# Making three quarters of two expert stages' norms in the attention stage ahead, and ending the expert blocks without GpSimd's drain

## The reference

```
def _layernorm(x, axis=-1, eps=1e-05):
    m = jnp.mean(x, axis=axis, keepdims=True)
    v = jnp.var(x, axis=axis, keepdims=True)
    return (x - m) / jnp.sqrt(v + eps)

x = x + _L0_xattn_ref(_layernorm(x), ctx, ctx, ...)   # 16 heads of 16 over ctx
x = x + _L0_ffn_ref(_layernorm(x), ...)               # experts choose tokens
x = x + _L1_xattn_ref(_layernorm(x), ctx, ctx, ...)   # 16 heads of 64 over ctx
x = x + _L1_ffn_ref(_layernorm(x), ...)               # each token's best 2 of 8 experts
x = x + _L2_xattn_ref(_layernorm(x), ctx)
x = x + _L2_ffn_ref(_layernorm(x), ...)               # quantised weights
x = x + _L3_xattn_ref(_layernorm(x), ctx, ctx, ...)
x = x + _L3_ffn_ref(_layernorm(x), ...)               # quantised inputs and weights
```

```
# _L0_ffn_ref: 16 experts, each takes its best 64 of 512 tokens
router_logits = jax.nn.silu(hidden_states @ router_w1) @ router_w2
expert_probs = jax.nn.softmax(router_logits.transpose(0, 2, 1), axis=-1)
expert_weights, token_indices = jax.lax.top_k(expert_probs, cap)
...
# _L1_ffn_ref: 8 experts of width 256 or 512
probs = jax.nn.sigmoid(logits.astype(jnp.float32))
topw, sel = jax.lax.top_k(probs, TOP_K)
```

## Time and profile before

| | before |
|---|---|
| median of 3 runs | 1683.46 us (1682.42 to 1688.7) |
| profiled execution: its own time | 1683.53 us |
| its span | 1681.7 us |
| mean granted TensorE clock | 0.918 |
| first VectorE work of f1 | 235.80 us |
| first VectorE work of a2 | 593.28 us |
| first work of f3 | 1014.15 us |
| first fetch of a4 | 1222.64 us |

### The profile page before, as it was taken

The page is one execution under the profiler, slowest core; times in us unless marked ns, Lnnn a source line. Parts: engine busy times, 40 slices in busy tenths (PEclk is TensorE's granted clock), DMA queues, the critical chain, the costliest instruction groups (busy, mean ns, idle before and its releaser), DMA issues. The chain is left out here.

```text
span 1681.7 us, 29336 instructions
## 1 busy us (share of the span) xinstructions
PE 1415.6 (84%) x9650; PEld 1138.7 (68%) x9650; DVE 1078.5 (64%) x2487; ACT 836.1 (50%) x1944; POOL 488.6 (29%) x428
## 2 busy tenths in 40 slices
PE   5899974999999749999999995699856897888885
PEld 4666542888888647888888873599744786555553
DVE  4677643666666537777787765644366753688886
ACT  2466541544544437666677764255423543455551
POOL 2112011577777610000000004255412311134343
PEclk8899876999999979999999997699978997799997
DMA  4322124456556345544554434122173002222110
GB/s 144 122 87 84 50 101 163 113 140 163 134 136 164 60 126 141 127 115 114 133 131 104 108 120 133 34 77 77 60 227 105 1 0 62 74 78 74 60 52 26
DMA packets 140109, 168.91 MB, mean 100 GB/s; under 512 B 20136, under 2 KB 131880, under 8 KB 137448
## 3 DMA queue, kind: packets, MB, share of 16 engines
q1 hardware_dynamic: 115000, 131.42, 26.7%
q0 software_dynamic: 16032, 27.01, 7.5%
q10 hardware_dynamic: 8976, 9.17, 1.8%
HBM read 75.66 MB, written 24.12 MB: 59 GB/s over the span
## 5 line engine op out<-in xcount | busy, mean ns | idle before, releaser
L1131 ACT ACTIVATE a_probT<-a_t 128x512 f32<-128x512 f32 x256 | 151.6, 602 | 164.6 <-PE a_t L860 138.5
L941 DVE TENSOR_REDUCE a_nmax<-a_s 128x2 f32<-128x512 f32 x256 | 170.9, 685 | 92.2 <-PE a_s L856 92.0
L63 POOL TENSOR_TENSOR a_rstd<-a_veps,minus_half 128x2 f32<-128x2 f32 x32 | 23.2, 724 | 507.1 <-DVE a_veps L57 507.1
L856 PE MATMUL a_s<-a_ka,a_qa 48*128 48x256 f32 x512 | 123.2, 342 | 44.8 <-DVE a_nmax L941 21.2
L856 PEld LDWEIGHTS a_s<-a_ka,a_qa 48*128 48x128 f32 x512 | 78.6, 202 | 105.3 <-issue 61.4
L441 DVE TENSOR_REDUCE a_nmax<-a_score 128x2 f32<-128x512 f32 x128 | 88.0, 687 | 86.7 <-PE a_score L334 86.6
L536 ACT ACTIVATE a_prob<-a_score,a_nmax 128x256 f32<-128x256 f32 x256 | 120.3, 481 | 34.4 <-DVE a_nmax L441 34.3
L1665 POOL DMA_INDIRECT x_rows<-f_hn,f_scatter_row x60 | 129.9, 2164 | 16.4 <-issue 16.4
L860 PE MATMUL a_t<-a_qa,a_ka 50*128 50x256 f32 x512 | 123.2, 339 | 2.2 <-DMA a_qa<-a_m_lo 1.2
L1608 ACT ACTIVATE f_gate<-f_gate 128x512 f32<-128x512 f32 x64 | 38.3, 599 | 129.0 <-PE f_gate L1411 111.0
L1521 DVE TENSOR_TENSOR f_y<-f_gate,f_value 128x512 f32<-128x512 f32 x64 | 44.0, 688 | 80.4 <-PE f_value L1411 78.4
(11 more groups left out here) (385 smaller groups left out, 4414.3 us busy)
## 6 DMA issues: line engine op xcount, KB each, us to landing
area_odd<-in_L_experts SPq DMA_DIRECT2D x15, 1536.0 KB, 6.8
a_k_hi<-a_k_fresh_hi SPq DMA_DIRECT2D x128, 128.0 KB, 2.4
a_ctxT<-in_ctxT SPq DMA_DIRECT2D x64, 128.0 KB, 2.6
a_ka<-a_k_hi SPq DMA_DIRECT2D x128, 64.0 KB, 2.6
a_k_lo<-a_k_fresh_lo SPq DMA_DIRECT2D x64, 128.0 KB, 2.4
a_q<-a_q_fresh_hi SPq DMA_DIRECT2D x64, 128.0 KB, 2.4
a_q<-a_q_fresh_lo SPq DMA_DIRECT2D x64, 128.0 KB, 2.4
a_qa<-a_q_hi SPq DMA_DIRECT2D x120, 64.0 KB, 2.6
```

Source lines behind the costliest of these rows:

```text
L856: last_s = nc.tensor.matmul(ps_s[i][:, half, :], qa[rows, u % RING, j, half * P:(half + 1) * P], ka[rows, u % RING, j, :], start=True, sto ...
L941: nc.vector.tensor_reduce(nmax[:, u % 2, :, i * PPU + j], ps_s[i][:, :, :], AX.X, ALU.max, negate=True).then_inc(sem["nmax"], 1)
L1131: nc.scalar.activation(probT[:, t % NPT, i, :, :], ps_t[i][:, :, :], ACT.Exp).then_inc(sem["exp"], 1)
```

## The change

1. The norms of groups 0 to 2 of f1 are made in a0's last batch: stats at steps T = 56, 59, 62, apply at 57, 60, 63, each behind what VectorE does in that step; the power on GpSimd, in the step of the stats. Those of f3 are made in a2's last batch: stats at s = 8, 10, 12, apply at s = 9, 11, 13. They go into buffers (`chip.early`) that overlay a0's and a2's own norm and context buffers, which the last batch has done with; the first stats wait for that. The x that is normed is complete for those groups, since batches 0 to 5 are added by then.
2. f1 and f3 norm group 3 alone. TensorE's transposes and SP's writes of h of groups 0 to 2 wait for nothing of the norm any more.
3. f1's three early roundings on ScalarE move from in front of the copies to behind `keep_hidden(0)`, `(1)` and `(2)`.
4. f3's twelve roundings get another order and place: one per group between copy and sigmoid, the other eight after the last sigmoid. VectorE's first two subtractions stand ahead of the first scores and after the last copy of a transpose. GpSimd's memsets come ahead of its power, and its six subtractions wait for one norm, not four, and by the new order.
5. The Blocks of f1 and f3 end without GpSimd's drain. `scatter_row`, which its last scatters read, moves out of f1's own buffers.
6. In a2 the buffer `fresh` is placed ahead of `k_hi`.

```diff
+def early_stats(nc, dve, chip, sem, g):
+    norm_stats(nc, dve, chip.x, sem, chip.early, g * GT, GT, g, g * GT)
+def early_rstd(nc, pool, chip, sem, g):
+    norm_rstd(nc, pool, chip, sem, chip.early, GT, g, g * GT)
+def early_apply(nc, dve, chip, sem, g):
+    norm_apply(nc, dve, chip.x, sem, chip.early, g * GT, GT, g, chip.early.hn[:, g * GT:(g + 1) * GT, :], sem["hn"], g * GT)
...
# a2, VectorE
+            def norms_ahead(s):
+                g, odd = divmod(s - NU // 2, 2)
+                if 0 <= g < chip.early_groups:
+                    if odd:
+                        early_apply(nc, dve, chip, e_sem, g)
+                    else:
+                        if g == 0:
+                            for what in "kq":
+                                dve.wait_ge(*placed(B - 1, what, NKQ - 1))
+                            dve.wait_ge(sem["vb"], B * NV)
+                        early_stats(nc, dve, chip, e_sem, g)
...
+                    if not more:
+                        norms_ahead(s)
...
# a2, GpSimd, behind its last norm_rstd
+            for g in range(chip.early_groups):
+                early_rstd(nc, pool, chip, e_sem, g)
...
# a0
+    NORMS_AHEAD = 8 * (B - 1)
+    def norms_ahead(T, at):
+        n, off = divmod(T - NORMS_AHEAD - at, 3)
+        return n if start and off == 0 and 0 <= n < chip.early_groups else None
...
# a0, VectorE
+                if norms_ahead(T, 0) is not None:
+                    g = norms_ahead(T, 0)
+                    if g == 0:
+                        for kind in "qkv":
+                            dve.wait_ge(sem[projected[kind]], B)
+                        dve.wait_ge(sem["ctx_lo"], B)
+                    early_stats(nc, dve, chip, e_sem, g)
+                if norms_ahead(T, 1) is not None:
+                    early_apply(nc, dve, chip, e_sem, norms_ahead(T, 1))
...
# f1 and f3
-        block = ctx.enter_context(nc.Block())
+        block = ctx.enter_context(nc.Block(no_gpsimd_drain=True))
...
# f1 and f3, SP and TensorE
-                sp.wait_ge(sem["hn"], g + 1)
+                if g >= E_G:
+                    sp.wait_ge(sem["hn"], g - E_G + 1)
...
# f1, ScalarE
-            for n in range(3):
-                high_weights(0, 0, n)
             keep_hT(0)
             for g in range(1, GROUPS):
                 keep_hT(g)
                 keep_hidden(g - 1)
+                high_weights(0, 0, g - 1)
...
# f3
+    ROUNDED = [0, 6, 1, 7, 2, 8, 3, 9, 4, 5, 10, 11]
...
# f3, VectorE
+            for g in range(E_G, GROUPS):
+                norm_stats(nc, dve, chip.x, sem, nb, g * GT, GT, g - E_G, g * GT)
+                norm_apply(nc, dve, chip.x, sem, nb, g * GT, GT, g - E_G, hn[:, g * GT:(g + 1) * GT, :], sem["hn"], g * GT)
+            low_weights(POOL_PIECES)
             keep_scores(0)
             keep_scores(1).then_inc(sem["score"], 1)
             dve.wait_ge(sem["hTp"], GROUPS * KC)
             nc.vector.tensor_copy(hT[:, 1, 1, :], ps_T[1][:, :]).then_inc(sem["hT_last"], 1)
-            for n in range(POOL_PIECES, POOL_PIECES + 2):
-                low_weights(n)
+            low_weights(POOL_PIECES + 1)
...
# f3, ScalarE
-            for n in range(3):
-                high_weights(n)
             for g in range(GROUPS):
                 keep_hT(g)
-                if g + 1 < GROUPS:
-                    high_weights(3 * g + 3)
+                high_weights(ROUNDED[g])
                 keep_scoreT(g)
-                if g + 1 < GROUPS:
-                    for n in range(3 * g + 4, 3 * g + 6):
-                        high_weights(n)
+            for n in ROUNDED[GROUPS:]:
+                high_weights(n)
...
# f3, GpSimd
             def low_weights(n):
-                pool.wait_ge(sem["W_hi"], n + 1)
+                pool.wait_ge(sem["W_hi"], ROUNDED.index(n) + 1)
...
-            pool.wait_ge(sem["hn"], GROUPS)
+            pool.wait_ge(sem["hn"], GROUPS - E_G)
...
+        chip.early_groups = GROUPS - 1
```

More of the change, by code:

```diff
@@ L72, in norm_apply, with early_norms @@
     last.then_inc(sem_out, 1)
+def early_norms(nc):
+    at = -(-nc.sbuf_base // 32) * 32
+    buf, words = Bufs(), 0
+    for name, shape in (("stats", [P, TILES, 6]), ("mv", [P, TILES, 2]), ("veps", [P, TILES]), ("rstd", [P, TILES]), ("hn", [P, TILES, D])):
+        size = 1
+        for n in shape[1:]:
+            size *= n
+        alias = nc.alloc_sbuf_tensor_at(f"early_{name}", shape, F32, offset=at + 4 * words)
+        if name == "stats":
+            buf.stats = alias
+        elif name == "mv":
+            buf.mv = alias
+        elif name == "veps":
+            buf.veps = alias
+        elif name == "rstd":
+            buf.rstd = alias
+        else:
+            buf.hn = alias
+        words += size
+    buf.words = words
+    return buf
+def early_stats(nc, dve, chip, sem, g):
[4 more added lines that the diff above has]
+    norm_apply(nc, dve, chip.x, sem, chip.early, g * GT, GT, g, chip.early.hn[:, g * GT:(g + 1) * GT, :], sem["hn"], g * GT)
 def stage_semaphores(nc, chip, stage, names):
@@ L182, in head_attention @@
         ctx_hi, ctx_lo = sb("ctx_hi", [P, KC, S], F32R), sb("ctx_lo", [P, KC, S], F32R)
+        fresh = {what: [sb(f"{what}_fresh_{n}", [P, CPR, S], F32R) for n in ("hi", "lo")] for what in "kq"}
         k_hi = sb("k_hi", [P, H, S], F32R)
@@ L185, in head_attention @@
         q2 = sb("q2", [P, H, S], F32R)
-        fresh = {what: [sb(f"{what}_fresh_{n}", [P, CPR, S], F32R) for n in ("hi", "lo")] for what in "kq"}
         vb = sb("vb", [P, TB, E])
@@ L701, in narrow_head_attention @@
                                "score nmax st exp pv osb qrow0 qrow1 qrow2 qrow3 krow0 krow1 krow2 krow3 mrow0 mrow1"
+                               + (" e_stats e_aggr e_veps e_rstd e_hn" if start else "")
                                + (" l_stats l_aggr l_veps l_rstd l_hn amax qscale iscale v grid unit low big t_ up upp step rows_ "
@@ L704, in narrow_head_attention @@
         l_sem = {name: sem["l_" + name] for name in "stats aggr veps rstd hn".split()} if linear else None
+        e_sem = {name: sem["e_" + name] for name in "stats aggr veps rstd hn".split()} if start else None
         projected = {"hT": "hTp", "q": "qp", "k": "kp", "v": "vp", "mT": "mTp", "OT": "OTp", "BT": "BTp", "out": "outp", "XT": "XTp", "lin": "linp"}
@@ L1293, in pb @@
             return ctx.enter_context(nc.psum_tensor(f"{stage}_{name}", shape, F32))
-        nb = norm_buffers(nc, ctx, stage, TILES)
-        hn = sb("hn", [P, TILES, D])
+        sb("early", [P, chip.early.words])
+        nb, hn = chip.early, chip.early.hn
+        E_G = chip.early_groups
         hT = sb("hT", [P, KC, B * S])
@@ L1684, in pair_of @@
                     scatter(q, not more and q == 1)
-            for g in range(GROUPS):
-                norm_rstd(nc, pool, chip, sem, nb, GT, g, g * GT)
+            for g in range(E_G, GROUPS):
+                norm_rstd(nc, pool, chip, sem, nb, GT, g - E_G, g * GT)
             pool.wait_ge(sem["next"], 1)
@@ L2159, in pb @@
             return ctx.enter_context(nc.psum_tensor(f"{stage}_{name}", shape, F32))
-        stats = sb("stats", [P, TILES, 6])
-        mv = sb("mv", [P, TILES, 2])
-        veps = sb("veps", [P, TILES])
-        rstd = sb("rstd", [P, TILES])
-        hn = sb("hn", [P, TILES, D])
+        sb("early", [P, chip.early.words])
+        nb, hn = chip.early, chip.early.hn
+        E_G = chip.early_groups
         hT = chip.spare_words.rearrange("p (q k s) -> p q k s", q=2, k=KC)
@@ L2353, in then @@
                 dve.wait_ge(sem["top"], step[0])
-            def statistics(g):
-                tiles = range(g * GT, (g + 1) * GT)
-                for t in tiles:
-                    last = nc.vector.bn_stats(stats[:, t, :], chip.x[:, t, :])
-                last.then_inc(sem["stats"], 1)
-                nc.vector.memset(veps[:, g * GT:(g + 1) * GT], EPS)
-                dve.wait_ge(sem["stats"], g + 1)
-                for t in tiles:
-                    last = nc.vector.bn_aggr(mv[:, t, :], stats[:, t, :])
-                last.then_inc(sem["aggr"], 1)
-                dve.wait_ge(sem["aggr"], g + 1)
-                these = slice(g * GT, (g + 1) * GT)
-                nc.vector.tensor_tensor(veps[:, these], veps[:, these], mv[:, these, 1], ALU.add).then_inc(sem["veps"], 1)
-            def normalise(g):
-                dve.wait_ge(sem["rstd"], g + 1)
-                for t in range(g * GT, (g + 1) * GT):
-                    last = nc.vector.tensor_scalar(hn[:, t, :], chip.x[:, t, :], mv[:, t, 0:1], rstd[:, t:t + 1], ALU.subtract, ALU.mult)
-                last.then_inc(sem["hn"], 1)
             def keep_scores(g):
@@ L2611, in _ @@
             nc.gpsimd.memset(ones[:, :], 1.0).then_inc(sem["cleared"], 1)
-            power(2)
-            power(3)
-            pool.wait_ge(sem["hn"], GROUPS)
+            for g in range(E_G, GROUPS):
+                norm_rstd(nc, pool, chip, sem, nb, GT, g - E_G, g * GT)
+            pool.wait_ge(sem["hn"], GROUPS - E_G)
```

41 lines of the change are left out of this document (18 added, 23 removed).

## The result

| | before | changed |
|---|---|---|
| median of 20 runs | 1685.99 us (1680.98 to 1699.39) | 1682.51 us (1674.66 to 1688.81) |
| profiled execution, span | 1681.7 us | 1673.5 us |
| mean granted TensorE clock in it | 0.918 | 0.925 |

The ratio of the changed kernel's times to those before is 0.9964, with a 95% interval of 0.9948 to 0.9979: -6.1 us, between -8.8 and -3.5. (The two medians alone are 3.5 us apart.) The prediction was -3.4, 1680.1 us with a range of 1669.5 to 1689. The median lies in that range, the gain has the forecast sign, and it is somewhat larger than forecast: -3.4 is just outside the measured interval. All ratios here are of fast executions; one of experiment 8's eight, of 2052.83 us at a granted clock of 0.634, is left out of its ratio.

The account below looks back on a forecast made before the run. With TensorE busy 84% and VectorE 64%, it judged each place by its own timeline, not by averages. From 1683.5 us, +4.0 -6.5 -5.1 +9.5 +0.0 -5.3 = -3.4 gave 1680.1 us, 8-in-10 range 1669.5 to 1689.

Parts of the forecast that it names:

- a0's end: End of the first attention: 9.66 us more VectorE work in eight steps, partly hidden in its idle time; +4.0 us.
- f1's front: Start of f1: transposes begin with the block because groups 0 to 2 are already normed; -6.5 us.
- f1's drain: End of f1: without GpSimd's drain the block's barrier is free sooner and a2 starts earlier; -5.1 us.
- a2's end: End of the second attention: 9.66 us of norms in six steps with only 0.6 us free on VectorE; +9.5 us.
- f3's front: Start of f3: scores 7.5 to 9.3 us earlier, but four GpSimd subtractions hold the choice of experts; 0.0 us.
- f3's drain: End of f3: without GpSimd's drain the next stage's fetch waits only for the scatter's landing; -5.3 us.
- Rival 1: f3's choice: small operations slip between GpSimd's pieces, so the front gives 8.5 us; -11.9, 1671.6 us; chance 0.22.
- Rival 3: Attention ends: added stops drop TensorE's clock to 0.50, a0 paying 8.5 and a2 13 us; +7.6, 1691.1 us; chance 0.07.
- Rival 2: Attention ends: TensorE and ScalarE run ahead during norms, a2 paying 4.8 and a0 1.1 us; -11.0, 1672.5 us; chance 0.06.
- Rival 4: Ends of f1 and f3: the next stage pays the drain's time as waits for landings or GpSimd; +7.0, 1690.5 us; chance 0.10.

Follow-up runs that it names:

- experiment 8: Changed kernel with only group 0 normed in a2's steps 8 and 9, groups 1 to 3 in f3; ratio to before 0.9922 (-13.2 us).
- experiment 6: Changed kernel with a0's norms alone moved to steps 64 to 71, a2 as changed; ratio to before 0.995 (-8.4 us).
- experiment 7: Changed kernel with GpSimd's drains back at the ends of f1 and f3; ratio to before 0.9997 (-0.5 us).
- 12: The kernel of 11 with GpSimd's drains kept in f1 and f3; ratio to before 0.9919 (-13.6 us).
- 11: Changed kernel, norms moved behind a0's and a2's last maxima (three groups each), GpSimd's f3 subtractions ahead of the choice; ratio to before 0.9861 (-23.4 us).
- 2: Changed kernel with GpSimd's subtractions 2 to 5 in f3 replaced by memsets of the same tensors; one execution, 1673.63 us.
- 3: Changed kernel with f3's roundings reordered, two per group, so GpSimd's six subtractions can run ahead of the choice; ratio to before 0.9934 (-11.1 us).
- experiment 1: Kernel before, with f1's and f3's Blocks ended without GpSimd's drain and `scatter_row` moved; ratio to before 0.999 (-1.7 us).
- 9: Kernel before, with f3's Block alone ended without GpSimd's drain; ratio to before 0.9997 (-0.5 us).
- 10: Kernel before, with f1's Block alone ended without GpSimd's drain; ratio to before 0.9995 (-0.8 us).

## Why the prediction was right, and where it wasn't

By its own steps, with what the profiles showed:

| step | predicted | measured | from |
|---|---|---|---|
| a0's end | +4.0 (1.1 to 8.4) | +5.8 in steps 56 to 63, +6.4 in a0 | means of 5 executions with and 9 without norms there |
| f1's front | -6.5 (-5.5 to -8.1) | -8.8 | the logits' maximum |
| f1's drain | -5.1 | -5.1 | scatter's end to a2 |
| a2's end | +9.5 (8 to 13) | +9.0 in its steps, +9.6 in a2 | changed against before (+10.5 by means of 5 executions with and 4 without norms) |
| f3's front | 0.0 (-1 to +2) | -4.4 (-3.1 in experiment 6) | the seventh operation |
| f3's drain | -5.3 | -5.2 | scatter to fetch |
| sum | -3.4 | 6.4-8.8-5.1+9.6-4.4-5.2 = -7.5 | timed: -6.1 (-8.8 to -3.5) |

The likeliest case came out, by its own mechanisms at each place, but the closeness of the sum owes something to luck: a0 cost 2.4 us more than forecast and the two fronts together gave 6.7 us more, and these errors partly cancel. Three terms hit within 0.3 us by the profiles: both drains and a2 (a2 within 1.0 by the means). There the price was read from a place with no slack (VectorE 9.17 of 9.78 us busy) or from a chain with one link, and experiment 8 shows the price per group. a2's six steps took 18.78 us in each of the five executions with three norms there, at clocks from 0.82 to 0.91, so the 0.5 us put on for the clock wasn't spent in them. The timed runs split the gain otherwise: the drains gave 5.6 us of the 10.4 (give or take about 5), and the norms ahead, forecast at +7.0, gave -0.5 (experiment 7). There too two errors cancel.

Two fronts were mis-sized, and the clock is in both. I costed the transposes and router products at the half clock of the earlier trace rows, 1.97 us a group, and took the fast clock as the upper end for f1 and not at all for f3. The clock was 1.00 at the start of both blocks in the kernel before too and fell while TensorE stood idle for the norm; with the norms ready it stayed at 1.00 for about 20 us, and a group took 1.06 us in both stages. In f3 the scores so came 12.0 us earlier where I had 7.5 to 9.3. The clock doesn't always stay up there. f1's front had 1.00 in all ten executions with norms ahead, f3's only in four; in the others it was at 0.50 for 3.4 to 6.8 us. Executions with the same front show what that costs: in experiment 6 the choice began at 19.4 us and its seventh operation at 29.0, where the changed kernel had 18.1 and 27.7, and in 12 (0.50 for 6.8 us) the choice began at 20.7 where 11 (3.4 us) had 18.7. The rest of that step held: four pieces of GpSimd's met the four operations with two SBUF inputs, and they cost 2.14+2.32+2.01+2.31-4x0.29 = 7.6 us. Rival 1, that small operations aren't held, is refuted, and experiments 2 and 3 show the cause: take the reads away, or the pieces from beside the choice, and 6.1 or 5.5 us come back at the gather. The Trainium skill's page "SBUF — State Buffer", section "Who interferes with whom", says that a VectorE instruction with two SBUF inputs contends with a GpSimd instruction that reads SBUF and not with one that only writes it, and that reductions never contend on this chip. The traces agree in each part: operations held for the rest of a whole instruction (up to 2.32 us), reductions not held (0.29), and no wait beside a memset (0.29).

a0's term was too small by 1.8 to 2.4 us. I took VectorE's idle time as spread evenly, 0.9 us a step. It isn't: before, it was nothing in steps 56 and 61, 0.7 to 0.8 in 57, 58 and 62, and 2.1 in 59 and 60. The first stats, in step 56, so delayed by their full 1.9 us. The clock was lower as well: the stretch ran at 0.78 where it had been 0.89 (0.78 to 0.81 in the five executions with norms in these steps, 0.89 to 1.00 in the nine without). How the 1.8 to 2.4 us divide between the two isn't shown. Rival 3 had this mechanism, and too much of it (8.5). Rival 2 (TensorE and ScalarE take the norms in) is refuted in a2 by 18.78 us. Rival 4 is refuted at its place, by the starts of a2 and of the fetch in every profile without drains.

What stays open is the drains' worth in the timed runs. In the kernel before, 10.3 us at the two ends show as 1.7, and by one drain each as 0.5 and 0.8 (experiments 1, 9, 10); in 11 against 12 they show as 9.8 and in 7 against the changed kernel as 5.6. The mean clock of each timed execution goes along with most of this scatter. Over the 69 executions of the kernel before in the experiments, the time falls by 1.2 us for each 0.001 of mean granted clock (correlation -0.90). Compared at the same clock by that slope, experiment 1 is 5.1 us faster than before, 9 and 10 are 2.2 and 2.3 faster, 7 is 2.6 slower, 11 is 15.9 and 12 is 10.2 faster, and the changed kernel 3.5, each give or take 1 to 1.5. So the two drains come out at 5.1 in the kernel before, at 5.7 in 11 against 12, and at about 6 in 7 against the changed kernel: nearly the same everywhere.

An estimate says that this comparison must come out below 10.3: the removed time was idle at a clock of 0.50 to 0.52 (588 to 593.2 and 1217.3 to 1222.5 of the kernel before), so leaving it out raises the mean clock by itself by some 0.0025, which the slope counts as 3 us. Against the 7 that then remain, 1 to 2 us aren't found. In experiments 1, 9 and 10 the mean clock wasn't higher but 0.001 to 0.002 lower than before; with 10 to 12 executions each, that can be chance, and whether an earlier stage shifts the clock of a later one these runs don't tell.

The change's net gain so is the drains'. The norms ahead brought 8.8 and 4.4 us at the fronts and cost 6.4 and 9.6 at the ends, +2.8 by the places; experiment 7 timed them at -0.5, with +2.8 inside its interval, and at the same clock at +2.6. In the tails they cost 0 to 1.2.

## What to carry to other kernels

Work that is moved ahead costs what the engine lacks at its new place: look for the stretch in which that engine waits, here behind the last maxima, and not for the earliest point at which the data are there. Look at it step by step: an average of the idle time hid that one step of a0 had none. Move only as much as the next stage's first products need; in f3 one group of three did nearly all. An engine that is given work at once may also keep a clock that it lost while it waited. When a stage's front gets shorter, look at what then runs beside the next chain: an engine that was done before may now hold it. An end-of-block drain is worth removing where it is the last thing that the barrier waits for, provided that whoever reads the data waits for their landing itself, as here; where it is over before, it costs nothing. And where the clock differs between executions, compare times at the same clock before calling a gain lost.

## What the runs showed of the hardware

- An operation of VectorE with two tensors in SBUF, 0.29 us by itself, takes up to 2.32 beside GpSimd subtractions of 2.35. The wait goes both ways: a GpSimd subtraction took 3.36 us where one of VectorE's, 1.2 by itself, came between. In the choice the engines took turns, one instruction each. Beside a memset of GpSimd (0.95 us) it takes 0.29.
- The same last stage, with equal busy times of VectorE, ScalarE and GpSimd, took from 276.7 to 288.4 us, with TensorE's mean granted clock at 0.88 and 0.84 in the two whose windows are shown. Over 69 executions of the kernel before, time and mean granted clock correlate at -0.90, 1.2 us for each 0.001.
- The granted clock was 1.00 at the start of f1 in the kernel before and in the changed one. It fell to 0.50 2.2 us into the block where TensorE had nothing to do for 5.4 us, and stayed at 1.00 for 20 us where TensorE began at once.
- GpSimd's drain took 13.1 and 7.7 us behind scatters, but it had no part in their landing: without it the rows of the last scatter were fetched 2.57 us after its issue.
